# Image 6 of a preactivated convolution block is copied out by rows, and its residual add is issued two additions sooner

## The reference

```python
def _gn(v):                      # each channel of each image has mean 0 and variance 1 afterwards
    return (v - mean(v)) / sqrt(var(v) + 1e-5)

def _L0_conv_ref(x, w1, w3, w5, w_proj):
    # the four parities of row and column become four groups of 32 channels: (8, 128, 32, 32)
    xd = concatenate([x[:, :, 0::2, 0::2], x[:, :, 0::2, 1::2], x[:, :, 1::2, 0::2], x[:, :, 1::2, 1::2]], axis=1)
    # depthwise convolutions of 1x1, 3x3 and 5x5, then a 1x1 projection of 384 channels to 128
    feats = concatenate([_dwconv(xd, w1, 1), _dwconv(xd, w3, 3), _dwconv(xd, w5, 5)], axis=1)
    y = einsum('bchw,oc->bohw', feats, w_proj)
    # the inverse of the first step: four groups of channels become the parities again
    out[:, :, 0::2, 0::2], out[:, :, 0::2, 1::2], out[:, :, 1::2, 0::2], out[:, :, 1::2, 1::2] = split(y, 4)
    return out

return x + _L0_conv_ref(_gn(x), w1, w3, w5, w_proj)
```

## Time and profile before

| what | value |
|---|---|
| median of 3 runs | 136.59 us |
| profiled execution, its own time | 135.8 us |
| its span, from first to last instruction | 134.0 us |
| busy: PE | 124.5 us, 93% |
| busy: DVE | 124.8 us, 93% |
| busy: POOL | 118.4 us, 88% |
| busy: ACT | 110.3 us, 82% |
| mean granted TensorE clock | 0.996 of full |

### The profile page before, as it was taken

How to read it: one execution, slowest core, us unless ns; L and a number is a source line. 1 busy time by engine, 2 the same in 40 slices (tenths; PEclk the granted TensorE clock), 3 DMA queues, 4 the chain that set the end, 5 groups by cost and what they waited for, 6 DMA issues and landing times.

```text
span 134.0 us, 1668 instructions
## 1 busy us (share of the span) xinstructions
PE 124.5 (93%) x514; PEld 96.5 (72%) x514; DVE 124.8 (93%) x234; ACT 110.3 (82%) x116; POOL 118.4 (88%) x92
## 2 busy tenths in 40 slices
PE   6968999999999999999999999999999999999900
PEld 6945888888886887688886788688688687588700
DVE  6679999999989999999999999999999999999950
ACT  2399979999999999999999999999999999160100
POOL 6279979999999999999999999999999999999730
PEclk9999999999999999999999999999999999999998
DMA  4999999980043008097999873978379995987696
GB/s 131 264 252 196 210 208 209 164 164 0 5 98 63 0 0 162 4 117 107 188 130 88 165 157 39 117 134 185 41 78 145 186 101 125 141 127 138 104 187 127
DMA packets 36024, 16.94 MB, mean 126 GB/s; under 512 B 34160, under 2 KB 34288, under 8 KB 35632
## 3 DMA queue, kind: packets, MB, share of 16 engines
q0 software_dynamic: 1568, 7.19, 39.8%
q1 hardware_dynamic: 32256, 8.98, 34.9%
q10 hardware_dynamic: 2192, 0.67, 2.1%
HBM read 5.46 MB, written 4.19 MB: 72 GB/s over the span
## 4 chain that ended last, share of the span: by engine, by line
PE 90%; DVE 5%; issue 1%; POOL 0%; DVEq 0%; POOLq 0%
PE YP L729 76%; PE YP L784 9%; PE YP L697 3%; DVE X L688 2%; DVE weff L606 1%; PE YP L794 1%; DVE HI L629 1%; PE YP L711 0%; POOL rstd L316 0%; DVE whi L614 0%; DVEq L105 0%; DVE agg L563 0%; DVE LO L532 0%; PE YP L717 0%; DVE nbias L570 0%
## 5 line engine op out<-in xcount | busy, mean ns | idle before, releaser
L347 POOL TENSOR_TENSOR RING_SUM<-RING_SUM,PROD 128x900 f32<-128x900 f32 (+1 forms) x45 | 93.3, 2079 | 3.3
L655 DVE SCALAR_TENSOR_TENSOR ACC<-G,coef,ACC 128x480 f32<-128x480 f32 (+3 forms) x132 | 82.0, 698 | 0.0
L480 ACT ACTIVATE PROD<-G,coef 128x900 f32<-128x900 f32 (+1 forms) x45 | 44.5, 1049 | 0.0
L729 PE MATMUL YP<-HI,whi 128*128 128x512 f32 (+1 forms) x146 | 36.6, 401 | 1.8 <-DVE HI L629 1.3
L729 PE MATMUL YP<-HI,wlo 128*128 128x512 f32 (+1 forms) x146 | 37.7, 410 | 0.0
L729 PE MATMUL YP<-LO,whi 128*128 128x512 f32 (+1 forms) x146 | 36.0, 398 | 0.0
L729 PEld LDWEIGHTS YP<-HI,whi 128*128 128x128 f32 x146 | 27.3, 189 | 9.2 <-DVE HI L629 1.4
L729 PEld LDWEIGHTS YP<-HI,wlo 128*128 128x128 f32 x146 | 27.5, 189 | 8.3 <-issue 2.4
L729 PEld LDWEIGHTS YP<-LO,whi 128*128 128x128 f32 x146 | 27.5, 189 | 6.7 <-issue 0.5
L442 ACT ACTIVATE G<-X,nbias,rstd 64x1024 f32<-64x1024 f32 x16 | 21.1, 1321 | 1.2 <-DVE nbias L570 0.9
L463 ACT ACTIVATE Y<-YP 64x1024 f32<-64x1024 f32 x14 | 15.4, 1097 | 3.3 <-PE YP L784 3.0
(11 more groups left out here) (69 smaller groups left out, 64.3 us busy)
## 6 DMA issues: line engine op xcount, KB each, us to landing
LO<-G POOLq DMA_DIRECT2D x7, 527.5 KB, 5.2
X<-in_x_dram SPq DMA_DIRECT2D x14, 256.0 KB, 5.5
X<-Y POOLq DMA_DIRECT2D x6, 512.0 KB, 7.2
out_dram<-X SPq DMA_DIRECT2D x12, 256.0 KB, 5.0
XS<-in_x_dram SPq DMA_DIRECT2D x1, 512.0 KB, 6.2
out_dram<-X SPq DMA_DIRECT2D x3, 128.0 KB, 2.4
X<-in_x_dram SPq DMA_DIRECT2D x2, 136.0 KB, 4.3
XS<-in_x_dram SPq DMA_DIRECT2D x1, 256.0 KB, 3.2
```

The costliest lines, as they stand in the source:

```text
L347: pool.tensor_tensor(dst, dst, prod(b, k), ALU.add).then_inc(prod_added, 1)
L480: act.activation(prod(b, k), g_tap(b, POOL_OF[b][k + 1]), ACT.Copy, scale=of5(POOL_OF[b][k + 1])).then_inc(prod_ready, 1)
L655: dve.scalar_tensor_tensor(half_part(ACC, tap, h), half_tap(b, tap, h), of5(tap), half_part(ACC, tap, h), ALU.mult, ALU.add).then_inc(acc_ ...
L729: mm = nc.tensor.matmul(dst, w[:, n, :], src, start=start, stop=False, skip_group_check=True)
```

## The change

The copies of image 6 from PSUM to Y are made first for rows 0 to 15 (both column parities) and then for rows 16 to 31 (both), in four instructions of 512 columns in place of two of 1024. The counter `y_copied` goes up with each of them. It stands at 14 when the upper half has been copied, which is what the DMA add of the upper half waits for, and at 16 after the lower half, which POOL's own addition of the lower half now waits for. The DMA add stands behind POOL's addition k = 3 of image 7 in place of k = 5.

```diff
-ADD_TOP6_AT = (7, 5)
+ADD_TOP6_AT = (7, 3)
...
-            pool.wait_ge(y_copied, 2 * (B - 1))
+            pool.wait_ge(y_copied, 2 * B)
...
-            def copy_y(b):
+            def copy_y(b, r0=0, r1=PH):
...
-                    act.activation(Y[p0:p0 + HALF, b // 2 % 2, :, :, j],
-                                   YP[HALF * j:HALF * (j + 1), b % AREAS, :].rearrange("p (h w) -> p h w", w=PW),
+                    act.activation(Y[p0:p0 + HALF, b // 2 % 2, r0:r1, :, j],
+                                   YP[HALF * j:HALF * (j + 1), b % AREAS, r0 * PW:r1 * PW].rearrange("p (h w) -> p h w", w=PW),
                                    ACT.Copy).then_inc(y_copied, 1)
...
-            copy_y(B - 2)
+            copy_y(B - 2, 0, BANK_ROWS)
+            copy_y(B - 2, BANK_ROWS, PH)
```

## The result

The changed kernel is slower. Over 20 runs of each it takes 136.95 us in the median, against 135.98 us for the kernel before: a ratio of 1.0074, with a 95% interval from 1.0050 to 1.0098, which is 1.0 us (0.7 to 1.3). On the 136.59 us that the prediction started from, that is 137.6 us. The forecast was 136.24 us, 0.35 us faster, with a range up to 137.2. The profiled execution of the changed kernel has a span of 134.8 us, against 134.0.

The account below looks back on a forecast made before the run. SP's queue of stores and the transfer speed were taken to bound the end, not arithmetic. Gains of 0.4 us by SP's issues and 0.3 us by transfers were averaged: 136.59 - 0.35 = 136.24 us, range 135.7 to 137.2.

Parts of the forecast that it names:

- What bounds the kernel: Kernel's end: SP's queue of stores and transfer speed set it, not arithmetic; SP's last store issues 1.45 us after last data.
- The copies by rows: ACT's copies of image 6: 0.64 us each, first pair done at 118.60; some 0.4 us extra on ACT, hidden.
- The DMA add two additions sooner: POOL, image 7: DMA issue at 118.68 after a 1.4 us stall; F 0.65 us later, lower half 1.42 us later.
- What the stores gain: Final stores: upper half goes early, five SP stores left from 128.00; end 0.35 us sooner, the mean of two estimates.
- (b): Final stores: POOL's 1.42 us stall reaches them in full, last issue at 131.42; 137.2 us; chance 0.22.
- (a): Final transfers: stores go at the mean 180 GB/s from 128.9 to 133.3, end moves +0.1; 136.7 us; chance 0.18.
- (c): Final stores: queues nearly empty, only last data count; 1.2 us less, 135.4 us; chance 0.13.
- (d): Image 6's DMA add: issued early, lands no sooner, at 126.8 after 8.1 us; 137.0 us; chance 0.07.

Follow-up runs that it names:

- the version with the wait alone: Changed kernel with POOL waiting for the upper half's copies behind k = 3 but issuing the DMA add behind k = 5; ratio 1.0073 against the kernel before.

## Why the prediction was wrong

**What bounds the kernel** was read rightly. SP is late because of the stores of the upper half: without them the kernel takes 1.0% less time. The forecast of 0.35 us faster failed on two terms that were mis-sized: the delay by POOL's stall, and what the stores gain in the end.

**The copies by rows** were right: 0.63 us for each was measured and 0.64 forecast, and they cost ACT nothing that matters.

**The DMA add two additions sooner** is the first step that failed, in size and not in kind. The mechanism was as forecast: POOL stands, F waits for POOL, all of F's delay arrives. But F came at 126.33 where I had 125.70, so that its delay was 1.28 us where I had 0.65 (from the first copy of image 6 it is 1.08 us). The lower half was added at 128.54 where I had 128.00. The terms, as they measured:
- image 6's result was ready 0.2 us later in this profile (117.50, not 117.30), and that is no part of the change;
- a DMA issue on POOL starts 0.30 us after the copy that it waits for ends (118.78 to 119.08). I had taken 0.08 us from an addition. In the version with the wait alone, where an addition waits, it is 0.08 again (118.99 to 119.07). That is 0.22 us missed;
- POOL's addition right after a DMA issue takes 2.29 us, not 2.02. In the rows of before that was k = 6, which nothing else in RING_SUM followed; I counted its length, but let k = 4 keep the short pitch of 2.16. It is now 2.43 (119.65 to 122.08), and the three take 6.59 us where I summed 6.42: 0.17 us missed.

The slack before F was 0.8 us. Once it is used up, every such term arrives in full: the last two make 0.4 us.

**What the stores gain** is the second step that failed, and the graver one. I had the last landing at 133.2, 0.4 us sooner than before; it came at 134.36, 0.7 us later. By parts:
- the five stores began at 128.57 and not at 128.00, which is the first step's error with the 0.2 us by which image 6 was later: 0.57 us;
- SP's issues followed each other by 0.65 us, where the middle that I took made 0.63: 0.1 us over the four. Counted from the first copy SP's last issue came at 13.68 us where I had 13.2;
- the last store took 3.1 us to land where I had 2.7, and it was ACT's, issued 0.06 us behind SP's: 0.5 us. ACT's queue, with the other store of the lower half, was not in the sum.

I wrote that the queue holds less than before, and so took the middle between short and long issues and between 180 and 221 GB/s. But the less that is in the queue here is what went out before; what remained did not go faster. From 129.40 on the 786 KB went at 186 GB/s for 4 us, close to the mean of the whole tail before, after 1.9 us in which nothing went. The lower half's SP store, which in the version with the add at k = 4 leaves 1.06 us ahead of image 7's quarters, now comes in one burst with them. So the forecast had the lower half's delay as a start time and not as bytes still to go when the last data are ready. With the lower half in time the last four issues take 0.3 to 0.4 us each, and the price of its delay is 1.2 us at the end of the profile, 1.3 us in the medians.

**The rivals.** (b) is what happened, in place and in sign: POOL's stall reached the end through the lower half. It had the last issue at 131.42, and 131.18 was measured. Its own mark, a mean issue interval above 0.7 us, would have missed it: the interval was 0.65 ((131.18 - 128.57) / 4). The other sign that I gave for it, a last issue after 130.8 though the upper half went early, was met. (a) was nearer to the truth than its chance: the engines were 91% busy at 186 GB/s from 129.40 to 133.40. What it had wrong is that the stall moves the end by only 0.1 us; the version with the add at k = 4 sends the same 786 KB in its last burst and ends 1.8 us sooner than before, since it sends them earlier. (c) did not hold for this kernel, but it is precisely the state of that version, where the last issue starts 0.03 us after the last data. (d) was wrong: the early add landed in 4.5 us. The chance of 0.26 for slower was too low: F's slack and the lower half both pointed one way, and I let a centre of opposite terms hide that the costs on POOL had been taken at their low ends.

## What to carry to other kernels

When a step with a wait is moved up an in-order queue, move it no further up than to the place at which its data are ready when the engine comes to it. Here, with the copies by rows, one addition earlier gave 1.3%, and two earlier cost 0.7%. Price every item that the stall pushes back, also one that no engine waits for, such as a store that falls in with the last burst. At the end of a kernel count the bytes that have still to go when the last data are ready, and look for stretches before in which the DMA engines move nothing. A slack read from one profile should be compared with the sum of small terms (a start after a wait, a longer first instruction) before it is called enough.

## What the hardware showed that I had not expected

- A DMA issue on POOL that waits for ACT starts 0.29 to 0.30 us after ACT's instruction ends, in all eight profiles in which it waits (118.78 to 119.08 in the changed kernel; 119.35 to 119.65 with the add at k = 3 alone; 120.48 to 120.78 with the add at k = 4 by parity). An addition on POOL starts after 0.08 us (118.99 to 119.07 in the version with the wait alone).
- The addition on POOL that follows the issue of image 6's add takes 2.28 to 2.30 us in all thirteen profiles, and others of the same shape 1.98 to 2.04.
- The issue of a store takes SP 0.32 us after a pause (128.57 in the changed kernel), up to 1.4 us behind others (1.35 us for the second store of the upper half in the version by rows with the add at k = 4), and in one case 3.30 us beside a running DMA add.
- TensorE's granted clock fell to 1.2 GHz in the last ring in the profile in which TensorE stood for 1.84 us before it, and not in the changed kernel's, in which it stood for 0.95 us. The last ring took 3.06 us in the one and 1.99 us in the other.
- When 550 KB or more are left at the last data, the end comes 4 us or more behind them; with 400 KB it comes 2.9 us behind (the column "left").
- Profiles differ in when image 6 begins, also two of the same kernel (117.06 and 117.75 in the version by rows with the add at k = 4, both with a clock of 1.00 between 10 and 20 us). The largest shifts come with a lower clock at the start: in the version by rows with the add at k = 5 the granted clock between 10 and 20 us is 0.83, where it is 1.00 in the kernel before, and image 6's copies start 1.0 us later (118.33). The three other profiles with 0.83 there have them at 118.2 to 118.4; that the clock is the cause was not tested. The stretch, in the version with the add at k = 5:

```profile
10.00:20.00 10.00, 9.54 (x36) 7.47 (x35) 8.94 (x20) 7.91 (x9) 7.70 (x9) 0.83 1.33 196
```
